# Attention and gated MLP in parallel: gate and up for 512 tokens at a time, with their product kept for a whole batch

## The reference

```
x  = input (16 batches, 512 tokens, 512 features);  xn = layernorm(x)
attention: qkv = xn @ w_qkv.T + b_qkv, 16 heads of 32, causal softmax, out @ w_out.T + b_out
mlp:  g = (xn @ gate_w.T) * gate_s          (1408 features)
      u = (xn @ up_w.T) * up_s
      down = (silu(g) * u) @ down_w.T * down_s
result = x + attention + mlp
```

## Time and profile before

| | us |
|---|---|
| median of 3 runs (lowest, highest) | 1941.18 (1940.52, 1946.4) |
| the profiled execution | 1942.44 |
| its span, first to last instruction | 1940.7 |
| busy share of the span: PE, PEld, DVE, ACT, POOL | 97%, 59%, 89%, 74%, 35% |

### The profile page before, as it was taken

One profiled execution on the slowest core, in us unless ns is written; L12 is line 12 of the kernel. 1 busy time (PEld: TensorE's weight loads), 2 busy tenths in 40 slices (PEclk: granted clock), 3 DMA queues, 4 the chain that ended last, 5 costly groups with the idle time before them and its releaser, 6 DMA issues.

```text
span 1940.7 us, 41614 instructions
## 1 busy us (share of the span) xinstructions
PE 1880.6 (97%) x14376; PEld 1153.6 (59%) x14376; DVE 1731.9 (89%) x5689; ACT 1445.7 (74%) x4153; POOL 679.5 (35%) x769
## 2 busy tenths in 40 slices
PE   7789999999999999999999999999999999999998
PEld 3445565665656656565665656656665665656655
DVE  7989999998898899998998898999998998898995
ACT  5668778787786877777787786777777787786873
POOL 3854151523324332332423324332332423312122
PEclk9989999999999999999999999999999999999999
DMA  9199999989888988988989888988988989888885
GB/s 314 40 182 147 168 163 161 174 137 180 138 141 167 152 164 137 162 147 160 165 138 175 144 142 169 148 166 139 161 147 161 166 137 177 143 127 161 132 159 97
DMA packets 805143, 300.32 MB, mean 155 GB/s; under 512 B 734144, under 2 KB 766912, under 8 KB 804928
## 3 DMA queue, kind: packets, MB, share of 16 engines
q1 hardware_dynamic: 804928, 297.62, 86.1%
HBM read 46.94 MB, written 16.78 MB: 33 GB/s over the span
## 4 chain that ended last, share of the span: by engine, by line
PE 57%; DVE 25%; DMA 8%; ACT 5%; SPq 2%; issue 1%; POOL 1%; ACTq 0%; DVEq 0%
PE psW L822 20%; PE psW L797 11%; PE psW L831 8%; DMA PT<-PL 8%; DVE PL L1161 7%; PE psW L813 7%; DVE psS L1145 6%; PE psS L885 5%; PE psW L899 4%; ACT PL L1302 3%; DVE small L1156 2%; DVE act_t L1139 2%; ACT psS L1288 2%; DVE act_t L1133 2%; PE psW L804 2%; SPq L746 1%
## 5 line engine op out<-in xcount | busy, mean ns | idle before, releaser
L822 PE MATMUL psW<-xT,Wgu 128*128 128x256 f16 x5632 | 675.1, 273 | 5.0 <-DVE act_t L1139 4.0
L1288 ACT ACTIVATE psS<-psS,small 128x512 f32<-128x512 f32 (+3 forms) x1024 | 524.3, 517 | 196.9 <-DVE small L1145 194.1
L822 PEld LDWEIGHTS psW<-xT,Wgu 128*128 128x128 f16 x5632 | 546.6, 98 | 101.5 <-DVE act_t L1139 5.0
L1145 DVE CUSTOM_DVE_ANT_0 psS<-psS,mask,small 128x512 f32<-128x512 f32 (+3 forms) x1024 | 536.2, 549 | 20.1 <-PE psS L885 18.7
L1378 POOL TENSOR_TENSOR hdn<-act_t,hdn 128x256 f16<-128x256 f32 x352 | 235.3, 672 | 818.2 <-ACT hdn L1283 816.4
L1161 DVE SCALAR_TENSOR_TENSOR PL<-psS,small,PL 128x256 f16<-128x256 f32 (+3 forms) x896 | 429.9, 514 | 51.2 <-ACT PL L1302 48.6
L1302 ACT ACTIVATE PL<-psS,small 128x256 f16<-128x256 f32 (+3 forms) x896 | 401.6, 523 | 96.9 <-DVE small L1156 59.0
L797 PE MATMUL psW<-xT,Wqkv 128*128 128x512 f16 x1536 | 358.6, 379 | 0.9 <-DVE Wqkv L990 0.9
L831 PE MATMUL psW<-Wdn,hdn 128*128 128x512 f16 x1408 | 323.7, 381 | 0.3 <-POOL hdn L1378 0.2
L885 PE MATMUL psS<-QK 96*128 96x512 f16 (+3 forms) x1024 | 251.0, 301 | 23.3 <-DVE PL L1161 19.6
L797 PEld LDWEIGHTS psW<-xT,Wqkv 128*128 128x128 f16 x1536 | 146.0, 97 | 157.7 <-issue 1.4
(11 more groups left out here) (147 smaller groups left out, 1713.2 us busy)
## 6 DMA issues: line engine op xcount, KB each, us to landing
QK<-PT SPq DMA_DIRECT2D x192, 256.0 KB, 5.8
y<-in_x SPq DMA_DIRECT2D x68, 256.0 KB, 3.5
out<-y SPq DMA_DIRECT2D x64, 256.0 KB, 4.6
xin<-in_x SPq DMA_DIRECT2D x60, 256.0 KB, 3.4
PT<-PL SPq DMA_TRANSPOSE x224, 5.5
...
```

Source lines behind the costliest of these rows:

```text
L822: mm = e.matmul(ps[:, 256 * up:256 * (up + 1)], Wgu[:, up, c, 128 * m:128 * (m + 1)], xT[b % 2][:, 4 * xl + c, 256 * hf:256 * (hf + 1)], s ...
L1145: e.tensor_tensor_reduce(s, s, mask[:, 512 - s.shape[1]:512], scale=negsc, scalar=BIG, op0=ALU.add, op1=ALU.min, accum_out=nmax[:, u % 16: ...
L1288: e.activation(s, s, ACT.Exp, bias=nmax[:, u % 16:u % 16 + 1], scale=-1.0, accum_out=rsum[:, u % 16:u % 16 + 1]).then_inc(sem["act exp"], 1)
```

## The change

Gate and up of 128 features become two items, `ga` and `up`, of 8 matmuls with 512 columns, each in a bank of its own; a unit now covers 512 tokens and there are 11 to a batch. The steps on DVE change places: `gate` forms (tanh+1) times gate as soon as the `ga` item is there, `up` multiplies by up and scale. `hdn` doubles to 512 tokens, `act_t` to 512 columns. The four `dn` items of a batch follow one another, after all 11 units. `hh` waits once a batch, for the last `dn` of the batch before. In batch 0 it waits for check 0 from unit 8 on, and not at all ahead of it.

Weights are staged elsewhere: gate part 0 in the end of `hdn`, gate part 1 and a down part in the (not yet written) output weights `Wo`, the output weights in `xT[1]` once check 6 is done. So `wo_hi` waits for checks 1 and 15, and `tr` of batch 1 for `wo_lo` and `bias`. Most down weights are loaded behind the first transfer of `QK`; their rounding and checks, the output weights and `bias` are due later. In `TIMES` the nominal values become up 650, gate 610, th 585, hh 520, hl 1150 ns. The scratch for dynamic DMAs is set to 1024 bytes.

```diff
+WO_AT = 60000
+WO_DUE = 80000
+BEFORE_PK = 4
+FFW_DN = 65000
+CHK = 40000
+CHK_STEP = 3000
...
-    def gate_up(self, due, b, hf, m):
-        k = b, hf, m
-        full = [("pe", "mm", ("dn", b, 1), 12)] if hf else [("pe", "mm", ("dn", b - 1, 3), 12)] if b else []
-        mm, end = self.item(due, "gu", *k, after=[("dve", "ffw", n, int(m >= 6)) for n in range(8)] + [self.transposed(4 * b + 2 * hf + t) for t in range(2)] + full)
+    def gate_up(self, due, b, m):
+        k = b, m
+        x_there = [self.transposed(4 * b + t) for t in range(4)]
+        full = [("pe", "mm", ("dn", b - 1, 3), 12)] if b else []
+        first, middle = self.item(due, "ga", *k, after=[("dve", "ffw", n, int(m >= 6)) for n in range(4)] + x_there + full)
+        second, end = self.item(middle, "up", *k, after=[("dve", "ffw", n, int(m >= 6)) for n in range(4, 8)] + [first])
...
-        self.add(end - EARLY, "act", ("th", *k), mm, ("dve", "ff_scales"), *free)
-        self.add(end - EARLY, "dve", ("up", *k), ("act", "th", *k))
-        self.add(end - EARLY, "dve", ("gate", *k), ("dve", "up", *k), ("dve", "ff_scales"))
-        empty = [("pe", "mm", ("dn", b, 1), 21)] if hf else [("pe", "mm", ("dn", b - 1, 3), 21)] if b else [("pe", "chk", 0), ("pe", "chk", 1)]
-        self.add(end, "act", ("hh", *k), ("dve", "gate", *k), *empty)
+        self.add(middle - EARLY, "act", ("th", *k), first, ("dve", "ff_scales"), *free)
+        self.add(middle - EARLY, "dve", ("gate", *k), ("act", "th", *k))
+        self.add(end - EARLY, "dve", ("up", *k), ("dve", "gate", *k), second, ("dve", "ff_scales"))
+        empty = [("pe", "mm", ("dn", b - 1, 3), 21)] if b else [("pe", "chk", 0)] if m >= 8 else []
+        self.add(end, "act", ("hh", *k), ("dve", "up", *k), *empty)
...
-        mm, end = self.item(due, "dn", b, t, after=[("dve", "ffw", m, 0) for m in range(8, 19)] + [("pe", "mm", ("red", "flag"), 1)] * (n == 0) + [("turn", "pe", "mm", ("gu", b, t // 2, NI - 1), 15)])
-        free = [("pool", "ya", n - 1)] if n else [("dve", "flag2"), *(("dve", "wqk_lo", s, r, 1) for s in range(2) for r in range(2))]
+        mm, end = self.item(due, "dn", b, t, after=[("dve", "ffw", m, 0) for m in range(8, 19)] + [("pe", "mm", ("red", "flag"), 1)] * (n == 0) + [("turn", "pe", "mm", ("up", b, NI - 1), 7)])
+        free = [("pool", "ya", n - 1)] if n else [("dve", "flag2"), ("act", "o_part", 3)]
...
-        free = [("pe", "mm", ("gu", b - 2, 1, NI - 1), 15)] if b >= 2 else [("pe", "chk", 6), ("pe", "chk", 15)]
+        free = [("pe", "mm", ("up", b - 2, NI - 1), 7)] if b >= 2 else [PE_BIAS, ("dve", "wo_lo", 3)]
...
-                free = [("pe", "pv", G - 1)] if G else [("pe", "chk", 12), *(("dve", "wqk_lo", s, 1, 3) for s in range(2)), ("dve", "wv_lo", 1), ("dve", "wo_lo", 3), PE_BIAS]
+                free = [("pe", "pv", G - 1)] if G else [("pe", "chk", 12), *(("dve", "wqk_lo", s, 1, 3) for s in range(2)), ("dve", "wv_lo", 1)]
...
+            free += [("turn", "sp", "pk", 0)] * (n - 8 >= BEFORE_PK)
...
-        self.add(70, "sp", ("bias_o",))
-        self.add(71, "sp", ("scale_d",))
+        self.add(70, "sp", ("bias_o",), ("turn", "sp", "pk", 0))
+        self.add(71, "sp", ("scale_d",), ("turn", "sp", "pk", 0))
...
-            self.add(80 + c, "sp", ("wo32", c), *(("dve", "wqk_lo", s, r, 2 + c // 2) for s in range(2) for r in range(2)))
+            self.add(WO_AT + c, "sp", ("wo32", c), ("pe", "chk", 6))
...
-            self.chain(48000 + c, "act", ("o_part", c), ("sp", "wo32", c), *(("dve", "wqk_lo", s, r, 1) for s in range(2) for r in range(2)))
+            self.chain(WO_DUE - 3000 + c, "act", ("o_part", c), *(("dve", "wqk_lo", s, r, 1) for s in range(2) for r in range(2)), ("sp", "wo32", c))
...
-        self.add(48500, "dve", ("o_max",), ("act", "o_part", 3))
-        self.add(49500, "dve", ("o_scales",), self.largest(49000, "o", ("dve", "o_max")), ("dve", "v_scales"))
+        self.add(WO_DUE - 2000, "dve", ("o_max",), ("act", "o_part", 3))
...
-            self.chain(50000 + c, "act", ("wo_hi", c), ("dve", "o_scales"))
-            self.chain(50000 + c, "dve", ("wo_lo", c), ("act", "wo_hi", c))
+            self.chain(WO_DUE + 2000 * c, "act", ("wo_hi", c), ("dve", "o_scales"), ("pe", "chk", 1), ("pe", "chk", 15))
+            self.chain(WO_DUE + 2000 * c, "dve", ("wo_lo", c), ("act", "wo_hi", c))
...
-        checks = {0: 34000, 1: 35000, 2: 38000, 3: 40000, 12: 42000, 8: 43000, 9: 44000, 10: 45000, 11: 46000, 5: 47000, 16: 48000, 4: 50000, 7: 52000, 13: 54000,
-                  14: 55000, 6: 56000, 15: 58000, 17: 59000, 18: 60000}
+        checks = {n: CHK + CHK_STEP * k for k, n in enumerate((2, 3, 0, 5, 4, 1, 7, 6))}
+        checks |= {n: FFW_DN + 4000 + 800 * k for k, n in enumerate((12, 16, 13, 14, 15, 8, 9, 10, 11, 17, 18))}
...
-                due = 22000 + 600 * n + 8000 * half if n < 8 else 38000 + 500 * (n - 8)
+                due = 22000 + 600 * n + 8000 * half if n < 8 else FFW_DN + 500 * (n - 8)
...
-            self.add(52000 + c, "sp", ("yl", c), ("pe", "chk", 8 + c))
-            self.add(56000 + c, "pool", ("yb", c), ("sp", "yl", c), ("dve", "bias"))
+            self.add(WO_DUE + c, "sp", ("yl", c), ("pe", "chk", 8 + c))
+            self.add(WO_DUE + 5000 + c, "pool", ("yb", c), ("sp", "yl", c), ("dve", "bias"))
...
-        self.item(50000, "bias", after=[("pool", "spread_bv")])
-        self.add(52000, "dve", ("bias",), PE_BIAS, ("sp", "bias_o"), ("sp", "scale_d"))
+        self.item(WO_DUE, "bias", after=[("pool", "spread_bv")])
+        self.add(WO_DUE + 2000, "dve", ("bias",), PE_BIAS, ("sp", "bias_o"), ("sp", "scale_d"))
...
-        gus = [(self.gate_up, hf, m) for hf in range(2) for m in range(NI)]
+        gus = [(self.gate_up, m) for m in range(NI)]
...
+        after = [qk(g) if b + 1 < NB else [] for g in (4, 5)]
...
-            seq = qk(2) + gus[0:4] + vs[0:2] + gus[4:5] + vs[2:4] + qk(3)
-            for k in range(6):
-                seq += gus[5 + k:6 + k] + os_[k - 1:k] * (k > 0)
+            seq = qk(2) + gus[0:2] + vs[0:2] + gus[2:3] + vs[2:4] + qk(3)
+            for k in range(3):
+                seq += gus[3 + k:4 + k] + os_[k:k + 1]
+            seq += after[0] + gus[6:7] + os_[3:4] + gus[7:11] + after[1] + dns
...
-            seq = vs + qk(0) + gus[0:4] + qk(1) + gus[4:8] + qk(2) + gus[8:11] + qk(3)
-        seq += (qk(4) if b + 1 < NB else []) + dns[0:2] + gus[11:17] + (qk(5) if b + 1 < NB else []) + gus[17:22] + dns[2:4]
-        costs = [(12 * 216, 12 * 216, 12 * 216, 16 * 109, 22 * 216)[(self.query_key, self.value, self.output, self.gate_up, self.down).index(s[0])] for s in seq]
+            seq = vs + qk(0) + gus[0:2] + qk(1) + gus[2:4] + qk(2) + gus[4:6] + qk(3) + gus[6:8] + after[0] + gus[8:11] + after[1] + dns
+        costs = [(12 * 216, 12 * 216, 12 * 216, 16 * 216, 22 * 216)[(self.query_key, self.value, self.output, self.gate_up, self.down).index(s[0])] for s in seq]
...
-    Wout = [sb(f"Wout{i}", [128, 4, D], F16) for i in range(2)]
+    Wo = sb("Wo", [128, 2, 4, D], F16)
...
-    hdn = sb("hdn", [128, NI, 2, 256], F16)
-    act_t = [sb(f"act_t{i}", [128, 256], F32) for i in range(3)]
+    hdn = sb("hdn", [128, NI, 2, 512], F16)
+    act_t = [sb(f"act_t{i}", [128, 512], F32) for i in range(3)]
...
+    Wout = [Wo[:, i, :, :] for i in range(2)]
...
+    Wo32 = [xT1f[:, 1024 * c:1024 * (c + 1)].bitcast(F32) for c in range(4)]
+    Wof = Wo[:, :, :, :].rearrange("p l c e -> p (l c e)")
...
-    ff_stage = [hdnf[:, 0:2 * F], hdnf[:, 2 * F:4 * F], PL[3][:, 0:2 * F], PL[2][:, 0:2 * F], PL3[:, 1024:1024 + 2 * F], QK1f[:, 0:2 * F], xT1f[:, 0:2 * F], oTf[:, 0:2 * F]]
-    dn_stage = [PTf[:, 0:1024], oTf[:, 2 * F:2 * F + 1024], oTf[:, 2 * F + 1024:2 * F + 2048], xT1f[:, 2 * F:2 * F + 1024], QK1f[:, 2 * F:2 * F + 1024]]
+    ff_stage = [hdnf[:, 6 * F:8 * F], Wof[:, 0:2 * F], PL[3][:, 0:2 * F], PL[2][:, 0:2 * F], PL3[:, 1024:1024 + 2 * F], QK1f[:, 0:2 * F], xT1f[:, 0:2 * F], oTf[:, 0:2 * F]]
+    dn_stage = [PTf[:, 0:1024], oTf[:, 2 * F:2 * F + 1024], oTf[:, 2 * F + 1024:2 * F + 2048], Wof[:, 2 * F:2 * F + 1024], QK1f[:, 2 * F:2 * F + 1024]]
...
-                    for s in range(2):
-                        for rest in range(2):
-                            sp.wait_ge(*done("dve", "wqk_lo", s, rest, 2 + n // 2))
+                    sp.wait_ge(*done("pe", "chk", 6))
...
-                        sp.wait_ge(*done("pe", "gu", b - 2, 1, NI - 1))
+                        sp.wait_ge(*done("pe", "up", b - 2, NI - 1))
...
-                        sp.wait_ge(*done("pe", "chk", 6))
-                        sp.wait_ge(*done("pe", "chk", 15))
+                        for c in range(4):
+                            sp.wait_ge(*done("dve", "wo_lo", c))
+                        sp.wait_ge(*done("pe", "bias"))
...
-                        for c in range(4):
-                            sp.wait_ge(*done("dve", "wo_lo", c))
-                        sp.wait_ge(*done("pe", "bias"))
...
-                elif kind == "gu":
```

(43 more changed lines are left out.)

27 lines of the change are left out of this document (12 added, 15 removed), and 6 rows, old and new, of the table TIMES.

## The result

| | us | ratio to the kernel before [95%] |
|---|---|---|
| before, median of 5 runs | 1941.18 | |
| after, median of 5 runs (1929.11 to 1932.21) | 1930.96 | 0.9938 [0.9921, 0.9954] |
| after, the profiled execution (its span) | 1932.21 (1930.4) | |

The change makes the kernel 10.2 us faster by the medians, 12 by the ratio with 9 to 15 in its interval. The forecast was 18 us, 1923; the sign and the range held, the size did not. The profiled executions differ by 10.2 us (1942.44 to 1932.21), so the two traces carry the whole difference.

What follows compares the result with a forecast made beforehand. PE was taken to bound the steady part, DVE next at 90%. Matmul work -7.3, small waits -5 and start -6, other terms 0, summed to -18.3 us: 1923 us from 1941.2, range 1902 to 1944.

Steps and rivals of the forecast that it cites:

- PE's own work: Gate and up matmuls: same columns, 2816 fewer matmuls, each saving a fixed 2 to 3 ns; -7.3 us.
- The durations: Wider gate and up steps: operation times worked out, giving DVE 34 us less work, ACT some 60, POOL 33.
- DVE's term: Gate and up on DVE: 34 us less work, but PE bounds the steady part and covers it; 0.
- The small waits: Steady part: PE's 29 us of short waits, put down to DVE emptying score banks late, barely shrink; -5 us.
- The start: First 200 us: fewer waits for checks, more gate and up open before the flag, DVE hardly relieved; -6 us.
- No `hh` waiting near 50 us: Sign in the start that the forecast is right: no `hh` waits for PE near 50 us.
- The port: Port shared by POOL and DVE: fewer but longer `hl` holds, 0 to 12 us more for DVE in its free time; 0.
- The order of a batch: Four `dn` in a row, next batch's `hh` waiting once; `qk` items and `act_t` buffers cover it; 0.
- the 126 from which it would have cost: Late-flag rival in batch 0: PE's extra work covers a flag up to about 126 us, then run slows; chance 0.13.
- Only the fixed part of the matmuls is won: Rival: small waits and start stay, only 7.3 us is won, 1934 us (1929 to 1940); chance 0.25.

Runs made afterwards that it cites:

- x1: Kernel after, with each gate and up matmul of 512 columns issued as two of 256 again, order of items kept: 1937.08 us, ratio 0.9975.
- x2: Kernel after, with the gate and up steps on DVE each issued as two operations of 256 columns: 1939.11 us, ratio 0.9987.
- x5: Kernel before, with a second copy of the three single probability buffers and a smaller scratch for dynamic DMAs: 1932.8 us, ratio 0.9949.
- x9: Kernel after, with SP's transpose of the 256-key tile ahead of the 512-key tile's from the third group on: 1920.82 us, ratio 0.9887.
- x11: Kernel before, with the order of transposes of x9: 1929.78 us, ratio 0.9937.
- x3: Kernel after, with units 6 to 10 of batch 0's gate and up waiting for the flag's product again: 1943.68 us, ratio 1.0009.
- x12: x10 with GpSimd's first four output-bias additions moved behind the last `hl` of batch 0: 1911.26 us, ratio 0.9829.
- x10: Kernel after, with x9's order of transposes, `pv` due 4 us earlier and the last batch's scores up to 6 us earlier: 1911.26 us, ratio 0.9836.
- x4: Kernel after, with `pv` due 4 us earlier (PV_LATE 9000 instead of 13000): 1924.79 us, ratio 0.9905.

## Why the prediction was right or wrong

*PE's own work*, -7.3: the trace shows -7.1, and x1 took back 6.1 to 7.2 us. The Trainium skill, TensorE: Matmul & The Clock Gate, section "Back-to-back issue gap", names two spacings for N = 512: 131 ns for a sustained stream of weight-load and matmul pairs, and about 216 ns by N/2.4 + 2.5 for a single one. This stream of such pairs runs at 215.6 ns, so the second holds here and the first does not.

*The durations:* 680 and 742 ns on DVE, 700 and 658 on ACT and 1157 on POOL were worked out, 679, 744, 698, 641 and 1162 measured. The busy time of POOL fell by 32 us over the run (33 expected) and that of ACT by 48 (some 60). DVE's fell by 26 and not by 34: over ten batches by 22.4, which is 2.2 a batch as expected, but in the first 200 us it rose by 5.2.

*DVE's term*, put at 0 since PE covers it: x2 says that undoing it costs 8 us. In the slower execution that was profiled most of the loss stood at 200 to 300 us, before the flag and at the end, where PE gave no cover. The step "none of the three bounds the steady part: the term by itself is 0" left out that a fixed order turns a longer operation into another list of waits.

*The small waits*, -5, "come from DVE being late with a score bank": this is the step that failed. The row named DVE as the releaser, and I took the engine named for the cause, without asking what DVE had waited for. x5, x9 and x11 show that 8 to 14 us of the 32 to 34 are a chain of `pv`, transposes, the single buffer of the 256-key tile, ACT and DVE, which a faster DVE does not touch: steady loss -1.9 with it, in place of -5. What the change wins there once the chain is gone stays open: from x11 to x9 the steady loss falls by 4.8 us, the size I gave, but x5, the kernel before with copies, stands at 20.3 us already, 0.5 below x9.

*The start*, -6: the net is -6.4 (12.4 won until 107 us, 6.0 given back by 300), which hits my number by luck: my reason for so small a number was that DVE is hardly relieved. In fact the idle PE was nearly halved, as x3 shows, and behind the flag a part comes back; by x3 both go together. x12 shows one place of that: POOL's bias additions, moved by the change beside the flag's operations, held DVE up, for 2.1 us of loss there and none of the run's time. What makes up the rest between 107 and 300 us, a wait of a `pv` of 2.2 us at 203 us among it, was not tried. "No `hh` waiting near 50 us" held, but one waited 8 us for DVE instead, behind a PE that stood 4.86 us at 52.5.

*The port*, 0: right in the steady part, where over ten batches the scale operations on 128x2 elements that the earlier trace rows show (L1156, L1162 after) took 226 ns on average, 241 before. In the first 200 us they took 523 ns where they had taken 430, and the mechanism was seen again in x10, at a place with followers. The Trainium skill, SBUF — State Buffer, section "Who interferes with whom", says of the port pair that whoever issues first holds it for the whole instruction, and counts `tensor_scalar` among the DVE operations that can need it; 1.15 us in x10 against 0.17 in x12 for the same TENSOR_SCALAR agrees.

*The order of a batch*, 0: wrong at the last one. With the four `dn` in a row no gate and up is left when the last group's transposes begin, and 9.7 us of PE's work lie over more than 14 us of them; where the kernel before had a `pv` right behind its `dn`, this one waits. x4, which puts 14.4 us of `dn` there, does not wait. I priced the block by what it does to DVE, and not by what PE would lack when no next batch follows: +5.8.

By the sum: work -7.1, steady -1.9, start -6.4, end +5.8, together -9.6; the other 0.7 of the spans' 10.3 lies ahead of the first matmul and behind the last. So the 8 us that the forecast was too low are the end (5.8) and the small waits (3.1). *The rivals:* the flag's product came at 110.84 us, short of the 126 from which it would have cost by my reckoning. That limit was too generous: the first `dn` stands at 116.27 us behind the last of batch 0's gate and up, so that some 5 us of slack were left behind the product, and not 15. "Only the fixed part of the matmuls is won" came nearest in its number, 1934, and not by its reason.
